# Two steps of the weighing of v at once, and q_aug and k_aug as a ring of half units

## What is computed

```python
x = x + 0.5 * ffn(layernorm(x))      # units 0 to 3
x = x + attn(layernorm(x))           # units 4 to 7
x = x + 0.5 * ffn(layernorm(x))      # units 8 to 11
```

```python
q, k, v = src @ Wq, src @ Wk_c @ Wk, src @ Wv_c @ Wv      # 16 heads of 8, q and k then rotated
sa = softmax(q @ k.T / sqrt(8)) @ v                        # per head, 512 by 512 scores
x = rmsnorm(src + sa @ Wo) * norm1_w
shared = swiglu(x @ W_shared_in) @ W_shared_out            # hidden width 256
h = swiglu(x @ W1_shared)
routed = sum(h @ W2_experts[e] * w[:, e] for e in range(8))   # w is zero but for the best 2 of one group
out = rmsnorm(x + shared + routed) * norm2_w
```

## Time and profile before

| | us |
|---|---|
| median of three runs | 874.33 |
| the profiled execution's own time | 874.73 |
| its span | 872.9 |
| PE busy | 811.1 |
| DVE busy | 673.0 |
| ACT busy | 497.3 |
| POOL busy | 332.5 |

### The profile page before, as it was taken

How to read it: one execution, slowest core, us unless ns; L and a number is a source line. 1 busy time by engine, 2 the same in 40 slices (tenths; PEclk the granted TensorE clock), 3 DMA queues, 4 the chain that set the end, 5 groups by cost and what they waited for, 6 DMA issues and landing times.

```text
span 872.9 us, 12671 instructions
## 1 busy us (share of the span) xinstructions
PE 811.1 (93%) x4144; PEld 294.9 (34%) x4144; DVE 673.0 (77%) x1296; ACT 497.3 (57%) x1042; POOL 332.5 (38%) x685
## 2 busy tenths in 40 slices
PE   3589999999999999999889999999999999999967
PEld 2133234433433332332313223233344343333333
DVE  5687998778759767876989998898987787682247
ACT  1045776356537645754777777767764575477320
POOL 2054325362543444345231613325153621522342
PEclk9578999999999999999999999999999999999989
DMA  3536232130120101010130331403311300000000
GB/s 103 154 85 148 73 63 54 27 72 3 46 32 1 39 11 32 6 43 12 21 76 6 76 77 39 101 16 92 59 39 36 83 10 1 4 13 3 1 12 13
DMA packets 27258, 38.92 MB, mean 45 GB/s; under 512 B 6949, under 2 KB 24965, under 8 KB 25573
## 3 DMA queue, kind: packets, MB, share of 16 engines
q1 hardware_dynamic: 25165, 36.39, 17.6%
q10 hardware_dynamic: 2028, 1.72, 0.8%
HBM read 28.01 MB, written 9.50 MB: 43 GB/s over the span
## 4 chain that ended last, share of the span: by engine, by line
PE 72%; DVE 18%; ACT 3%; issue 2%; DMA 2%; POOL 2%; ACTq 0%; POOLq 0%; SPq 0%; DVEq 0%
PE ps_out L682 17%; PE ps L668 14%; PE ps L649 13%; PE ps L744 11%; DVE maxes L820 11%; PE ps L729 6%; PE ps L631 2%; ACT probs L984 2%; PE ps L736 1%; PE ps L638 1%; DVE src L898 1%; PE ps L707 1%; DVE stats L779 1%; PE ps L720 1%; DVE src L791 1%
## 5 line engine op out<-in xcount | busy, mean ns | idle before, releaser
L984 ACT ACTIVATE probs<-ps 128x512 f32<-128x512 f32 x768 | 417.0, 597 | 249.3 <-PE ps L668 247.0
L820 DVE TENSOR_REDUCE maxes<-ps 128x1 f32<-128x512 f32 x768 | 482.9, 683 | 75.9 <-PE ps L649 74.2
L649 PE MATMUL ps<-k_aug,q_aug 72*128 72x512 bf16 (+1 forms) x768 | 259.6, 390 | 18.9 <-DMA k_aug<-ones_row 17.0
L668 PE MATMUL ps<-q_aug,k_aug 75*128 75x512 bf16 (+1 forms) x768 | 263.2, 383 | 5.3 <-DMA q_aug<-max_parts_rows 3.3
L682 PE MATMUL ps_out<-probs,v_aug 128*18 128x512 f32 x1536 | 203.1, 601 | 5.4 <-ACT probs L984 4.9
L649 PEld LDWEIGHTS ps<-k_aug,q_aug 72*128 72x128 bf16 (+1 forms) x768 | 66.0, 98 | 193.3 <-issue 123.3
L668 PEld LDWEIGHTS ps<-q_aug,k_aug 75*128 75x128 bf16 (+1 forms) x768 | 66.4, 97 | 149.9 <-issue 94.5
L744 PE MATMUL ps<-w,hidden 128*128 128x512 f32 x256 | 117.0, 596 | 0.0
L911 DVE TENSOR_TENSOR prod<-ps,gate 128x512 f32<-128x512 f32 x56 | 38.7, 692 | 58.3 <-PE ps L744 42.6
L1170 POOL TENSOR_TENSOR prod<-prod 128x512 f32<-128x512 f32 x28 | 35.5, 1268 | 97.0 <-DVE prod L911 93.8
L744 PEld LDWEIGHTS ps<-w,hidden 128*128 128x128 f32 x256 | 47.6, 190 | 51.3 <-issue 46.8
(11 more groups left out here) (121 smaller groups left out, 665.9 us busy)
## 6 DMA issues: line engine op xcount, KB each, us to landing
q_aug<-qk_parts SPq DMA_DIRECT2D x7, 1152.0 KB
k_aug<-qk_parts SPq DMA_DIRECT2D x21, 384.0 KB
qk_parts<-parts SPq DMA_DIRECT2D x45, 128.0 KB, 2.3
q_aug<-qk_parts SPq DMA_DIRECT2D x8, 288.0 KB
k_aug<-qk_parts SPq DMA_DIRECT2D x24, 96.0 KB
qk_parts<-parts SPq DMA_DIRECT2D x24, 64.0 KB, 2.0
q_aug<-qk_parts SPq DMA_DIRECT2D x12, 96.0 KB
k_aug<-qk_parts ACTq DMA_DIRECT2D x12, 96.0 KB
```

Source lines behind the costliest of these rows:

```text
L649: pe.matmul(bank(use[0]), q_aug[p0:p1, r, at, qt * 128:(qt + 1) * 128], k_aug[p0:p1, r, at, :], start=True, stop=True).then_inc(bank_full[ ...
L668: pe.matmul(bank(use[0]), k_aug[p0:p1, r, at, kt * 128:(kt + 1) * 128], q_aug[p0:p1, r, at, :], start=True, stop=True).then_inc(bank_full[ ...
L820: dve.tensor_reduce(maxes[:, u % 2, qt, h:h + 1], full(use[0]), AX.X, ALU.max)\
L984: act.activation(probs[:, step % P_RING, c, :], full(use[0]), ACT.Exp, scale=scale)\
```

## The change

- **`DOUBLE_UNITS = {1, 2, 3, 9, 10, 11}`.** In these units `weigh_v` is planned for every second step and does two steps, 16 instructions in one run. They are the ffn units that have experts of the unit before beside them. `P_RING` goes from 2 to 4 steps.
- **Half units.** `q_aug` and `k_aug` become rings of five halves of 8 heads (`HALVES_RING`), where they were rings of three units. A load (`stack`) is now planned for q and for k of each half, and the loads of the second half wait for the exponentials of the half five before. `v_aug` keeps three.
- **`EARLY_UNITS = {0, 1, 5, 6, 7, 8}`.** Units 5 to 8 have their maxima sent back in four pieces, where it was two.
- **Tables.** `MAX_LATE`, the `PREP` and `POST` tables and `HOLD` have new values, with tables of their own for more units. `Banks` keeps its counts in another form. `max_run` and `exp_run` could join two score tiles in one instruction, but `MAX_PAIRS` and `EXP_PAIRS` are empty, so they give 1 everywhere.

```diff
-AUG_RING = 3
+HALVES_RING = 5
+V_RING = 3
+MAX_PAIRS = set()
+EXP_PAIRS = set()
-P_RING = 2
+P_RING = 4
+DOUBLE_UNITS = {1,2,3,9,10,11}
-EARLY_UNITS = {0, 1}
+EARLY_UNITS = {0, 1, 5, 6, 7, 8}
...
-PREP = {"norm_stats": [0], "norm_apply": [10], "x_transpose": [13], "qk_project": [19, 35], "qk_split": [31, 45],
-        "v_project": [27], "stack": [42, 56]}
+PREP = {"norm_stats": [0], "norm_apply": [10], "x_transpose": [13], "qk_project": [19, 35], "qk_split": [35, 48],
+        "v_project": [31], "stack": [41, 48, 50, 51]}
...
-MAX_LATE = [39, 36, 23, 12, 16, 18, 22, 19, 17, 15, 17, 20, 22]
+MAX_LATE = [39, 33, 23, 14, 16, 18, 22, 24, 25, 21, 18, 18, 22]
...
-    return steps + [(at["stack"][qk], ("stack", u, qk)) for qk in range(2)]
+    return steps + [(at["stack"][2 * half + qk], ("stack", u, qk, half)) for half in range(2) for qk in range(2)]
...
-        for s in range(TILES // 4):
+        for s in range(steps_at_once(u) - 1, TILES // 4, steps_at_once(u)):
             late = u * TILES + 4 * s + 3 + WEIGH_LATE
             put(late, "weigh_v", u, s)
...
-                    qk, = args
-                    if u >= AUG_RING:
-                        pe_done(sp, "exp_scores", u - AUG_RING, TILES // 4 - 1, 3)
-                    load_rows(sp, u, qk)
+                    qk, half = args
+                    before_it = 2 * u + half - HALVES_RING
+                    if before_it >= 0:
+                        pe_done(sp, "exp_scores", before_it // 2, TILES // 8 * (before_it % 2 + 1) - 1, 4 - exp_run(before_it // 2))
+                    load_rows(sp, u, qk, half)
...
                 elif name == "weigh_v":
-                    s, = args
-                    taken(pe, "exp_scores", u, s, 3)
+                    last, = args
+                    taken(pe, "exp_scores", u, last, 4 - exp_run(u))
...
+                    for s in range(last - steps_at_once(u) + 1, last + 1):
+                        g, kt, n = s // TT, s % TT, u * 16 + s
...
+                        for c in range(4):
+                            x0 = VW * (g % 2)
+                            mm = pe.matmul(ps_out[COL * c:COL * c + 2 * VW, :],
+                                           v_aug[:, r, kt, 4 * (g // 2) + c, x0:x0 + 2 * VW],
+                                           probs[:, n % P_RING, c, :], start=first_one, stop=last_one)
+                        mm.then_inc(out_done, 1)
```

More of the change, by code:

```diff
@@ L147, in __init__ @@
     def __init__(self):
-        self.uses = [0] * BANKS
+        self.filled = [0] * BANKS
+        self.signals = [0] * BANKS
+        self.released = [None] * BANKS
         self.free_at = [0] * BANKS
[L151 to L159, removed]
@@ L174, with take @@
-POST_ATTN = {"heads_out": [3, 6], "heads_transpose": [11], "out_project": [15], "attn_out": [24]}
-POST_LAST_BUT_ONE = {"heads_out": [4, 4], "heads_transpose": [7], "out_project": [10], "rms_stats": [11, 73],
+    def take(self, name, u, place):
+        run = max_run(u) if name == "max_scores" else exp_run(u) if name == "exp_scores" else 1
+        n = 2 if name in TWO_BANKS else run if name in HOLD else 0
+        taken = sorted(sorted(range(BANKS), key=lambda i: self.free_at[i])[:n])
+        uses = []
+        for i in taken:
+            self.free_at[i] = max(place * 10, self.free_at[i]) + HOLD[name]
+            signal = taken[0] if run > 1 else i
+            if signal == i:
+                self.signals[i] += 1
+            uses.append((i, self.filled[i], self.released[i], (signal, self.signals[signal])))
+            self.filled[i] += 1
+        for i, _, _, then in uses:
+            self.released[i] = then
+        return uses
@@ L275, in plan @@
             name, u = step[0], step[1]
-            use = banks.take(name, place)
+            use = banks.take(name, u, place)
             out.append((name, u, step[2:], use))
@@ L516, in store_parts, with load_rows @@
                     .then_inc(parts_stored[qk], 16)
-        def load_rows(queue, u, qk):
+        def load_rows(queue, u, qk, half):
             queue.wait_ge(parts_stored[qk], PARTS * 16 * (u + 1))
[L521 to L529, removed]
-                        .then_inc(landed, 16)
[L531 to L541, removed]
@@ new lines, in load_piece @@
+        def load_piece(queue, u, qk, r0, of, r, at, n, landed):
+            d = head_dim(u)
+            if qk == 0 and u:
+                of = of.rearrange("c d h n -> (c d) h n").unsqueeze(1)
+                queue.dma_start(q_aug[r0:r0 + product_rows(u), r, at, :], of.to_broadcast([PARTS * d, PARTS, n, S]))\
+                    .then_inc(landed, 16)
+            elif qk == 0:
+                for s in range(PARTS):
+                    queue.dma_start(q_aug[s:product_rows(u):PARTS, r, at, :], of.rearrange("c d h n -> (c d) h n"))\
+                        .then_inc(landed, 16)
+            else:
+                for s in range(PARTS):
+                    r1 = r0 + PARTS * d * s
+                    queue.dma_start(k_aug[r1:r1 + PARTS * d, r, at, :], of.rearrange("d c h n -> (d c) h n"))\
@@ L542, in load_rows @@
                         .then_inc(landed, 16)
+                r1 = r0 + product_rows(u)
+                queue.dma_start(k_aug[r1:r1 + PARTS, r, at, :], ones_row[:, :, :].to_broadcast([PARTS, n, S]))\
+                    .then_inc(landed, 16)
         @block.sync
@@ L983, in _ @@
                         act.wait_ge(out_done, step - P_RING + 1)
-                    act.activation(probs[:, step % P_RING, c, :], full(use[0]), ACT.Exp, scale=scale)\
+                    act.activation(probs[:, step % P_RING, c:c + exp_run(u), :], both(use), ACT.Exp, scale=scale)\
                        .then_inc(bank_free[use[0][0]], 1)
```

230 lines of the change are left out of this document (147 added, 83 removed).

## The result

The changed kernel takes 912.1 us (four runs, 907.2 to 921.0) against 874.0 us before. The ratio is 1.0417, with a 95% interval of 1.0372 to 1.0462: 4.2% slower. The ratio leaves out the longest run, 921.0 us, whose mean granted clock was 0.932 where the other three had 0.946 to 0.953. The forecast was 868 us, a gain.

What follows compares the result with a forecast made beforehand. PE was taken to bound most stages, with neither PE nor DVE leading in stage 5. Pairs -10.1, fewer ACT waits -0.8, maxima -4.1 and queued loads +8.4 gave -6.6 us: 868 us, own range 864 to 873, 8 in 10 within 857 to 877.

Steps and rivals of the forecast that it cites:

- The worth of a pair: Weighing in six units: two steps per block pay PE's 0.21 us turnover once, 10.1 us less; bounds nothing and 10.1.
- The price that I named for that case: Without cover from banks and spare time, DVE would lose up to 0.9 us per pair, in stage 1 first.
- the sign that it fails by: Prediction fails if head waits are absent or over 5 us each, or DVE or ACT lacks tiles and PE waits.
- The waits at the heads of the stages: Heads of stages 2, 9 and 10: maxima queue behind 1.82 MB of loads; 8.4 us taken from 5.3 to 22.1.
- The choice of the low end: 8.4 us for the three waits, about 1 us above each low end, because one such load began at 229 GB/s.
- The wait in stage 0: Third piece of maxima stands behind half of unit 1's loads, about 1 us of slack; counted as nothing.
- The maxima's places: New maxima places and four pieces: -5 in stage 5, -1.8 in stage 6, +1.3 tiles, +1.4 transposes, together -4.1 us.
- about 46: Stage 5, 51.10 us before, should last about 46 us.
- where 1.2 was said: Stage 8 was to grow by 1.2 us, for four tiles and one transpose.
- The rule on tiling modes: Changing the tiling mode, not just the tile, drains TensorE; so a pair's second step pays nothing, the upper bound.
- The rival on the slower side: Queue at its slow end, 139 to 150 GB/s: waits at heads of stages 2, 9, 10 reach 22.1 us, 881.4 us; chance 0.10.

Runs made afterwards that it cites:

- first move of loads: Changed kernel with ffn prep's loads of k's first half and of q's and k's second halves moved behind the maxima's store and load: 889.0 us, ratio 1.0139.
- base kernel: Changed kernel with single weighing steps and the loads behind the maxima, in ffn prep and for unit 1: 868.9 us, ratio 0.9931 to the kernel before.
- the run with the old values: Base kernel with MAX_LATE and EARLY_UNITS as in the kernel before: 887.9 us, ratio 1.0141.
- the run with single steps alone: Changed kernel with DOUBLE_UNITS empty, one weighing step at a time, everything else as changed: 896.3 us, ratio 1.0227.
- unit 8 with pairs: Base kernel with pairs in all sixteen steps of unit 8 alone, whose stage has no experts: 873.4 us, ratio 0.9971.
- the run with two buffers: Base kernel with a ring of two buffers of probs in place of four (P_RING = 2): 868.8 us, ratio 0.9916.

## Why the prediction was wrong, step by step

- **The worth of a pair failed.** The step was "48 x 0.21 = 10.1 us less", with "seven banks and their spare time in these stages cover it". The turnover is saved, as the timeline shows. The cover is not there: the pairs cost 14.9 us where 10.1 us were to be gained, all of it where score tiles follow each other without experts between. I took DVE's spare time from the mean of a stage, 12 to 17 us. In the kernel before DVE is busy for 85% to 93% of the first 32 places of stages 1, 2, 3, 9 and 10, and for 66% to 77% of the other 32 (the halves of stage 10 are below). Between two blocks of pairs lie eight places with two tiles each, a run of sixteen, and there are seven banks. The price that I named for that case, up to 0.9 us per pair, is 24 x 0.9 = 22 us for the first halves, and was left out of the range. That the clock would fall with it was not foreseen at all; the estimate above gives it 8.5 of the 14.9 us. The prediction did name the sign that it fails by: DVE or ACT lacks tiles and PE waits for a bank.

```profile
692.70:724.30 31.60, 31.25 (x173) 12.61 (x172) 27.40 (x52) 22.70 (x51) 9.84 (x33) 1.00 0.14 29
724.30:764.10 39.80, 39.80 (x181) 15.30 (x179) 27.15 (x45) 18.80 (x42) 14.17 (x27) 1.00 0.01 2
```

- **The waits at the heads of the stages were right in place and mechanism, and too small.** I put 8.4 us on stages 1, 8 and 9, out of a range of 5.3 to 22.1. At the ends of these stages the next matmul starts 4.5, 6.5 and 7.9 us later than a plain step would have it, 18.9 in sum. From first load to landing it is 13.1 us in stage 1 and 15.1 in stage 9, where I had counted about 11. The choice of the low end rested on one window of 229 GB/s in the earlier trace rows; the whole transfer of the earlier trace rows gives 3.5 + 12 us, close to the 15.1 us of stage 9. The Trainium skill, "DMA: Bandwidth & Descriptors", Bandwidth, Measured, has 1 MB in 6.15 us, 341 GB/s, for 128 partitions and DMAs issued from GpSimd. These loads of 72 rows, issued by SP, ran well below it: 1.82 MB and the small store took 13.1 and 15.1 us.
- **The wait in stage 0** was counted at nothing with "about 1 us of slack". It is 3.6 to 3.8 us by itself, and without it stage 0 is 5.2 us shorter. The median fell by 5.2 us too, from one series of runs to another; by the two ratios to the kernel before it is 3.2 us.
- **What a wait does to the clock** had no term. In the changed kernel each of the four waits brings a stretch at the 1.2 GHz level. The two at the ends of stages 8 and 9 last 10.2 us each, 8.5 and 4.7 us of them after the wait. The first move of loads took away waits of 18.4 us (4.3 + 6.4 + 7.7) and 18.2 us of work at half speed after them (5.0 + 8.5 + 4.7), which lose 9.1 us. The kernel with the loads behind has three stretches of 3.4 us of its own in stages 2, 9 and 10, 5.1 us. By this estimate the move gives 18.4 + 9.1 - 5.1 = 22.4 us, against 23.1 measured; the other low stretches of the two kernels are left out of it. The move in stage 0, with single steps, took away a wait of 3.6 us and 3.4 us at half speed: 5.3 us, against 5.2.
- **The maxima's places**: -4.1 us fits what was measured, and is not shown by itself. The base kernel, which has them and neither pairs nor late maxima, is 5 to 7 us faster than the one before, and it has all the other new places too. Stage 5 went to 47.9 us where "about 46" was said, and stage 8 grew by 1.6 us where 1.2 was said. How much is due to the maxima and how much to the other new places is open; the run with the old values does not settle it.
- **The rule on tiling modes** (the Trainium skill, "TensorEngine Tiling (Array Packing)", Key Properties) held: the second step of a pair pays no turnover (1.85 us for sixteen instructions, 0.98 us for eight). What the longer block does to DVE and ACT was for me to work out.
- **The rival on the slower side** named the right mechanism, the queue, and gave 881 us. The changed kernel went beyond it, because the pairs and the clock came on top. Undone one after the other, the loads gave 23.1 us, the pairs 14.9 and unit 1's loads 5.2, from 912.1 down to 868.9. These steps add up by construction; that the first two do not depend on each other's order is what the run with single steps alone shows (15.9 us for the pairs, 22.1 us then for the loads).

## What to carry to other kernels

- A turnover saved on a full engine is worth its time only if what that engine feeds can take the work in larger lumps. Here a run of sixteen tiles, 0.22 us apart, met seven banks and consumers of 0.55 to 0.61 us per tile. Compare these in the part of the stage where the run falls, and not with the idle time over the whole stage.
- Ask of every small transfer on the critical path which large ones stand before it in the same queue, and count their bytes at the rate of a whole transfer in the trace. Moving a load behind the small one cost nothing here and gave back 23 us.
- A step added to an in-order list on one engine can stop three others, as the piece of maxima ahead of a split did. Price a stall on PE above its own length where the traces show the clock falling with it, as they do at all four long waits here.

## What the runs showed of the hardware that was not expected

- After the waits of 3.8 to 7.7 us the granted clock stayed at 0.50 for 4.7 to 8.5 us of work, and not longest after the longest wait. It fell near short waits too: in unit 8 with pairs after one of 1.15 us for a bank, where the window from 581 to 584 us shows 0.67, and at the start of stage 10 with pairs after two of 0.47 and 0.36 us (rows above).
- The clock also fell without a comparable wait. In the profiled execution of the kernel with unit 1's loads behind it stood low for 17 us in stage 2 (windows below, 0.54), with PE busy all the while and no wait above 0.2 us in the 4 us before. Stage 2 took 85.5 us instead of 77.4. The same stage in the run with two buffers took 79.0, with 3.4 us of low clock at the same place. What sets this off is open. A single profile of these kernels can be off by several us for it, so the totals above are medians; the lengths of single stages come from one profile each.

```profile
190.00:205.00 15.00, 14.04 (x82) 5.87 (x81) 13.87 (x35) 10.10 (x26) 4.04 (x9) 0.98 0.02 6
205.00:223.00 18.00, 18.00 (x59) 6.62 (x59) 7.88 (x13) 7.59 (x14) 8.15 (x27) 0.54 0.04 12
```

- The kernel before has such a stretch late in its span as well, beside those near its start: 6.8 us from 837.7 us on, while the last unit is finished (window below, 0.62).

```profile
837.00:846.00 9.00, 5.62 (x17) 3.31 (x18) 3.71 (x8) 1.19 (x2) 1.65 (x2) 0.62 0.10 29
```
